# Two orders inside one pipelined block: where TensorE's convolution pieces stand, and which engine takes one tap of a depthwise convolution

## The reference

```python
pooled = x.mean((2, 3))
dyn = _ln(pooled @ w_fc1.T, ln1_w, ln1_b) @ w_fc2.T        # one 5x5 kernel for each image and channel
out = depthwise_conv5x5(x, dyn)
out = ln2_w * (out - mean_c(out)) * rsqrt(var_c(out) + 1e-6) + ln2_b
out = gelu(einsum('bchw,oc->bohw', out, w_expand))         # 64 -> 256 channels
gx = sqrt(sum_hw(out ** 2)); nx = gx / (gx.mean(1) + 1e-6)
out = gamma * (out * nx) + beta + out
out = einsum('bohw,co->bchw', out, w_shrink) + x           # 256 -> 64 channels
```

## Time and profile before

| | |
|---|---|
| median of three runs | 835.85 us |
| the profiled execution | 835.57 us |
| its span, first to last instruction | 833.8 us |
| scans | about 502 us |
| block, from the first pooled sum to the end | about 331 us |
| slots 6 to 14 of the block, on VectorE | 617.6 to 780.6 us |
| busy share TensorE / VectorE / ScalarE / GpSimd | 93% / 75% / 48% / 54% |

### The profile page before, as it was taken

One profiled execution on the slowest core, in us unless ns is written; L12 is line 12 of the kernel. 1 busy time (PEld: TensorE's weight loads), 2 busy tenths in 40 slices (PEclk: granted clock), 3 DMA queues, 4 the chain that ended last, 5 costly groups with the idle time before them and its releaser, 6 DMA issues. The chain is left out here.

```text
span 833.8 us, 15628 instructions
## 1 busy us (share of the span) xinstructions
PE 777.4 (93%) x5399; PEld 637.8 (76%) x5399; DVE 626.8 (75%) x1143; ACT 400.5 (48%) x491; POOL 450.0 (54%) x450
## 2 busy tenths in 40 slices
PE   5999999999999999999999997878899999999887
PEld 5999998999998999999999996644445444444332
DVE  4666666666666666667888888999899999999955
ACT  5591002777773000000000005459889999999981
POOL 2333333333332333335888884977778877888510
PEclk9999999999999999999999996989899999999999
DMA  6770000000000000000000002122233343433234
GB/s 145 158 178 0 0 0 1 1 0 0 0 0 1 1 0 0 0 0 1 1 0 0 0 0 50 32 75 78 53 79 82 85 104 97 103 79 80 58 74 102
DMA packets 61571, 35.81 MB, mean 43 GB/s; under 512 B 41504, under 2 KB 59488, under 8 KB 61536
## 3 DMA queue, kind: packets, MB, share of 16 engines
q1 hardware_dynamic: 59424, 34.83, 17.6%
q10 hardware_dynamic: 2112, 0.52, 0.3%
HBM read 17.85 MB, written 9.37 MB: 33 GB/s over the span
## 5 line engine op out<-in xcount | busy, mean ns | idle before, releaser
L504 PE MATMUL psum<-line_hi,taps_hi 128*128 128x256 f32 x1270 | 202.9, 292 | 11.7 <-DVE taps_lo L400 8.5
L518 PE MATMUL psum<-line_lo,taps_hi 128*128 128x256 f32 x1270 | 202.5, 291 | 0.8 <-DVE line_lo L453 0.8
L512 PE MATMUL psum<-line_hi,taps_lo 128*128 128x256 f32 x1270 | 202.0, 291 | 0.0
L453 DVE SCALAR_TENSOR_TENSOR line_lo<-psum,rest 128x256 fp32r<-128x256 f32 x254 | 108.2, 426 | 123.6 <-POOL rest L285 115.3
L504 PEld LDWEIGHTS psum<-line_hi,taps_hi 128*128 128x128 f32 x1270 | 177.0, 192 | 12.9 <-issue 9.2
L518 PEld LDWEIGHTS psum<-line_lo,taps_hi 128*128 128x128 f32 x1270 | 176.4, 191 | 1.9 <-DVE line_lo L453 1.7
L512 PEld LDWEIGHTS psum<-line_hi,taps_lo 128*128 128x128 f32 x1270 | 176.7, 191 | 0.0
L285 POOL TENSOR_TENSOR rest<-x,line_hi 128x256 f32<-128x256 f32 x127 | 82.8, 652 | 168.3 <-DVE line_hi L444 168.3
L793 POOL TENSOR_TENSOR part<-part,prod 128x1008 f32<-128x1008 f32 (+2 forms) x56 | 127.4, 2274 | 17.1 <-ACT prod L860 11.3
L285 POOL TENSOR_TENSOR rest<-by_h,line_hi 128x256 f32<-128x256 f32 x127 | 91.5, 720 | 83.4 <-DVE line_hi L444 83.4
L337 ACT ACTIVATE by_h<-x (+1 forms) x128 | 85.7, 669 | 105.8 <-DVE x L433 104.1
(11 more groups left out here) (159 smaller groups left out, 763.1 us busy)
## 6 DMA issues: line engine op xcount, KB each, us to landing
stage<-in_x_dram SPq DMA_DIRECT2D x32, 256.0 KB, 4.1
rstd_wide<-rstd_dram SPq DMA_DIRECT2D x30, 256.0 KB, 5.4
out_dram<-x SPq DMA_DIRECT2D x28, 256.0 KB, 5.5
crossed<-x SPq DMA_DIRECT2D x16, 256.0 KB, 3.5
crossed<-x SPq DMA_DIRECT2D x16, 240.0 KB, 3.3
rstd_dram<-rstd SPq DMA_DIRECT2D x15, 64.0 KB, 1.5
out_dram<-x ACTq DMA_DIRECT2D x4, 128.0 KB, 4.6
out_dram<-x SPq DMA_DIRECT2D x4, 128.0 KB, 3.9
```

Of the source, the lines that this page charges most:

```text
L453: dve.scalar_tensor_tensor(out=line_lo[:, (slot + 1) % SLOTS, :, part], in0=as_lines(line_ps[slot][:, 0:LINE]), scalar=0.0, in1=as_lines(r ...
L504: mm = pe.matmul(line_ps[slot][:, 0:LINE], taps_hi[:, s, d, :], line_hi[:, slot, :, d:d + WP], start=(d == 0), stop=(d == OFFSETS - 1))
L512: pe.matmul(line_ps[slot][:, 0:LINE], taps_lo[:, s, d, :], line_hi[:, slot, :, d:d + WP], start=False, stop=False, skip_group_check=True)
L518: mm = pe.matmul(line_ps[slot][:, 0:LINE], taps_hi[:, s, d, :], line_lo[:, slot, :, d:d + WP], start=False, stop=(d == OFFSETS - 1), skip_ ...
```

## The change

It has two parts. On TensorE, in every slot, piece 1 moves from ahead of the statistics to behind shrink 1, and piece 3 from ahead of expansion (0,1) to behind it. The two pieces of ten products that stood together thus become piece 0 alone, pieces 1 and 2 together, and piece 3 alone. The number of products is the same. Second, `EARLY` shrinks to the units 3, 4 and 5: units 6, 8, 10, 12 and 14 go back to ten VectorE taps and five products (five more instructions of L860 and of L793, five fewer of L996), and VectorE takes one tap, never two, between finish 1 and the response.

```diff
-EARLY, EARLY_TAP = (3, 4, 5, 6, 8, 10, 12, 14,), ("up", 3)
+EARLY, EARLY_TAP = (3, 4, 5,), ("up", 3)
...
                 if v >= 0:
                     finish(v, 1)
-                take(1 + len(dve_taps(s)) - len(DVE_TAPS))
+                take(1)
                 if n in range(UNITS) and n % 2 == 1:
                     respond(n // 2)
...
                 at_v(0)
                 conv(0)
-                conv(1)
                 if w in range(UNITS):
                     statistics(w)
                 at_e(0, 0)
                 at_v(1)
+                conv(1)
                 conv(2)
+                at_e(0, 1)
                 conv(3)
-                at_e(0, 1)
                 if n in range(UNITS) and n % 2 == 1:
                     respond(n // 2)
                 at_e(1, 0)
```

## The result

The changed kernel takes 829.0 us, the median of four runs (828.85 to 830.81), against 835.42 for the kernel before, measured beside it. The ratio is 0.992, 95% interval 0.991 to 0.993: 0.8% faster, twice what the forecast of 832.6 had, and 0.5 us under its range. The profiled execution took 829.11, its span is 827.4.

A forecast was written before the change was run, and what follows sets the result against it. The prediction took a ring of waits between nearly full engines to bound the kernel. Gains of 2.6 us in the early slots and 0.4 in the steady ones, 3.0 in all, took 835.57 to 832.6; range 829.5 to 835.6.

The forecast's parts named there:

- the ring: Steady slots: a closed chain of waits between VectorE, ScalarE and TensorE sets a pair's length, 35.9 us against 36.0.
- The respond of slot 6 ... 2.6 us earlier.: Early slots: VectorE's respond in slot 6 starts at 627.9, against 630.49 before, a gain of 2.6 us.
- The other half of the step, the statistics: Slots 1 and 2: statistics one piece earlier remove VectorE's pauses for the squared mean, 1.7 us.
- rival A: Slot 3: TensorE's clock stays high, its last piece ends about 1.3 us earlier, 831.3 us in all; chance 0.13.
- The steady slots ... 0.1 us a pair.: Slots 6 to 14: each pair takes 35.9 for 36.0 us, four pairs gaining 0.4 us.
- The tail ... shifts with it, unchanged.: After slot 15: the tail hangs on VectorE's last unit and only shifts with it, no gain of its own.
- The tap ... buys nothing on the path.: Steady slots: VectorE's freed tap, 1.21 us, turns into a wait for TensorE's response, no gain on the path.
- The pause ahead of the respond: Sign, slots 4 to 14: VectorE newly waits 1.5 to 2 us for TensorE's response ahead of L1070.
- the added product: Steady slots: a fifth product in even units adds 1.0 us to ScalarE's part of the chain of waits.
- Rival B: Steady slots: only TensorE's idle time matters, a pair takes 34.1 us, 825.4 us in all; chance 0.06.
- Rival C: Steady slots: single pieces and the later response cost 0.35 us more a pair, 834.0 us in all; chance 0.20.
- Rival D: Steady slots: two pauses in odd slots drop TensorE's clock, 1.6 us a pair, 839.0 us in all; chance 0.09.

The follow-up runs named there:

- run 8: The kernel before with thirteen matmuls of no use added in each of slots 3 and 4, in TensorE's pauses; 832.1 us, ratio 0.9959.
- comparison 5: The changed kernel measured once more, nothing altered, beside the other versions; 829.95 us, ratio 0.9928 to the kernel before.
- run 6: The changed kernel with TensorE's response put ahead of piece 3 in even slots; 822.7 us, ratio 0.9844 to the kernel before.
- run 11: The changed kernel with TensorE's response ahead of piece 3, measured once more; 822.6 us, ratio 0.9836 to the kernel before.
- run 2: The kernel before with the taps and products of the change alone, TensorE's order as before; 836.3 us, ratio 1.0009.
- run 1: The kernel before with the new order of TensorE's pieces alone, taps and products as before; 827.5 us, ratio 0.9911.
- run 4: The kernel before with piece 3 alone moved behind expansion (0,1); 834.7 us, ratio 0.9995.
- run 7: The kernel before with the new order of TensorE's pieces, taps as before, and the response ahead of piece 3; 823.2 us, ratio 0.9847.
- run 10: The changed kernel with the response ahead of piece 3 and a second tap ahead of VectorE's respond in slot 4; 823.0 us, ratio 0.9835.

## Why the prediction was wrong

Its direction was right, and the ring it describes is there. Its sizes were not: 6.4 us came where 3.0 were forecast, 2.0 more in the early slots, 0.8 more in the steady ones and 0.6 in the tail. By its own terms:

- **"The respond of slot 6 ... 2.6 us earlier."** This step failed: it came 4.6 earlier. It goes wrong at expansion (0,1) of slot 4. The step took the half clock of slot 3 as it was and put that expansion at 587.74; it started at 586.09, 1.65 earlier still. Of these, 0.3 were there at the end of slot 2, and the other 1.35 came in slot 3, where expansion (1,0) took 1.13 for 2.08 and the products behind it ran at the full clock. The 1.65 are there again at the respond of slot 4 (588.98, forecast 590.7) and make up all but 0.3 of the miss at slot 6 (625.93, forecast 627.9). The other half of the step, the statistics, was about right: 1.9 at the end of slot 2 where 1.7 were forecast, though the pause in slot 1 was not the order's alone, as run 8 shows. The clock was put down as rival A, with a chance of 0.13 and a price of 1.3 us, from slot 3 alone. In this kernel that is what it gave; in the kernel before, where nothing else moves and the half clock of slot 4 shows too, it is worth 3.8. The reason against A was that TensorE's idle time is spread and not shortened. The rows say that it is shortened: 0.94 and 0.52 for 0.95 and 1.90 in slot 3, 1.56 and 0.17 for 1.22 and 1.36 in slot 4.
- **"The steady slots ... 0.1 us a pair."** The ring is the one described, and was mis-sized. Forecast 12.31 + 13.9 + 9.45 + 0.2 = 35.9; measured from respond to variance 12.36, root to the end of the square 13.82, statistics to the end of the response 9.39, signals 0.11 in all: 35.68. Against a difference of 0.3 these small excesses were two thirds of the effect. Four pairs gave 1.2, not 0.4. What the forecast did not see is the second path of the same length, through expansion (1,0) and TensorE's work behind it (comparison 5).
- **"The tail ... shifts with it, unchanged."** It lost another 0.6 us. The shrink ahead of the last statistics, behind the same pause of 2.44, ran at the half clock in the kernel before and at the full one after, here in this order:

```profile
796.11 3.48 PE L1312 MATMUL psum<-wide,shrink_now 128*64 128x512 f32 x8 [2.44 <-DVE x L1090]
```

```profile
790.36 1.94 PE L1312 MATMUL psum<-wide,shrink_now 128*64 128x512 f32 x8 [2.44 <-DVE x L1090]
```

  To the next respond this gave 1.1; in the stretch behind it 0.35 went back, as in every profile with one tap fewer. The clock there is partly chance: one and the same kernel, runs 6 and 11, has this shrink at 3.46 and at 1.94.

- **"The tap ... buys nothing on the path."** Right. The pause ahead of the respond was forecast at 1.5 to 2 us and is 1.89 from slot 8 on (2.02 in slot 4, 1.11 in slot 6); run 2 shows the tap's 1.21 turned into 1.23 of waiting. That the added product costs about 1.0 in ScalarE's part is right too, 0.97, but leaving it out (run 1) shortens the pair by 0.05 only, because TensorE's path is as long.
- **Rival B** (a pair of 34.1, no pause ahead of the respond) was not this change, but one more move away: run 6 took the response out of the ring and came to 34.51. The Trainium skill (Perfetto Trace Analysis, section Optimization Strategies) says to optimise the engines that block the critical path when the matmul engine idles. The traces agree only when the chain is followed on: TensorE's own waits, 0.80 and 0.51, are for ScalarE's gelu, and what paid was VectorE's wait, for TensorE.
- **Rival C** did not come. TensorE's busy time in a pair rose from 34.1 to 34.4, so the single pieces may cost 0.3, but its part of the ring did not grow (9.39 for a forecast 9.45).
- **Rival D** did not come either. The granted clock is 1.00 over the pair, with pauses of 0.80 and 0.51. It took a sum of pauses of 2.6 for the point that decides, and the runs show no such point: slot 3 of run 4 kept the full clock behind 2.15 and 0.51, slot 4 of run 7 fell behind a single 1.58. The Trainium skill (Perfetto Trace Analysis, section Matmul Optimizations) says that the matmul engine scales its power with utilization, so that matmuls should run back to back in batches. Here the smaller batches came with the higher clock, 1.00 for 0.85 over the stretch from 566 to 600.

The range missed by 0.5 us. Its lower end had A, at 1.3 where the early slots gave 2.0 more than the sum, and nothing for the tail.

## What to carry to other kernels

Where several engines are nearly full, add up the closed chain of waits, link by link, to the hundredth, look for a second chain of the same length, and ask of each moved instruction which link it lengthens: here a half-microsecond response stood behind a piece of 1.28 us, and moving it past that piece gave as much as the whole change. When an engine is relieved and a pause of the same length appears ahead of its next wait, the relief was not on the path. And where a profile shows a stretch of TensorE at the half clock, price it by filling the pauses ahead of it with matmuls of no use before you price anything else in those slots. Count the positions of two profiles from a common instruction near the place, not from the start of the span: here that was 0.8 of 4.6 us.

## What was not expected of the hardware

In the kernel before TensorE fell to the half clock, 1.2 GHz, behind two pauses of 0.95 and 1.90 us, and again behind 1.22 and 1.36, none as long as two microseconds. In the changed kernel it stayed up behind 0.94 and 0.52, and 1.56 and 0.17. The length of the pauses alone does not decide it: it stayed up behind 2.15 and 0.51 (run 4, slot 3) and fell behind a single 1.58 (slot 4 of runs 7 and 11), where runs 6 and 10, with the same order on TensorE and the same pause to within 0.02, stayed up. Thirteen 128x128 matmuls in each of slots 3 and 4, results unused, made the kernel before 0.4% faster. Behind one and the same pause of 2.44 us in the tail the clock fell in one profile and not in the other. Single executions of one kernel differ by up to 4.3 us (piece 3 alone).
